# Batch-axis attention: who writes the weight blocks, and which engine forms the normalised rows

## The reference

```python
def _L1_attn_ref(query, ...):           # query: L=16, N=128, E=256
    H = 16; L, N, E = query.shape; d = 16; scale = d ** (-0.5)
    q = split_heads(query @ q_proj.T + q_bias) * scale      # (N, H, L, d)
    k = split_heads(query @ k_proj.T + k_bias)
    v = split_heads(query @ v_proj.T + v_bias)
    scores = einsum('nhld,nhkd->nhlk', q, k)
    scores = where(tril(ones((L, L))), scores, -10000.0)
    attn = softmax(scores, axis=-1)
    ctx = einsum('nhlk,nhkd->nhld', attn, v)
    return ctx.transpose(2, 0, 1, 3).reshape(L, N, 256) @ out_proj.T + out_bias
```

## Time and profile before

| | us |
|---|---|
| device time, three runs | 1278.31, 1285.85, 1287.44 (median 1285.85) |
| profiled execution, its own time | 1279.03 |
| its span in the trace | 1277.2 |
| the batch-axis block in it | from about 712 to 848 |
| of it, the weighing: start of the lane writes to the end of the last strip | 789.0 to 816.8 |
| of it, the output projection and normalisations | 817.7 to 848.2 |

### The profile page before, as it was taken

The page is one execution under the profiler, slowest core; times in us unless marked ns, Lnnn a source line. Parts: engine busy times, 40 slices in busy tenths (PEclk is TensorE's granted clock), DMA queues, the critical chain, the costliest instruction groups (busy, mean ns, idle before and its releaser), DMA issues. The chain is left out here.

```text
span 1277.2 us, 23930 instructions
## 1 busy us (share of the span) xinstructions
PE 1136.4 (89%) x8865; PEld 731.3 (57%) x8880; DVE 909.6 (71%) x2118; ACT 570.3 (45%) x1521; POOL 283.8 (22%) x343
## 2 busy tenths in 40 slices
PE   9799999899998999889899987779999999879965
PEld 3587888677763333335456545657777776334422
DVE  1799999599995787848997598654458778843325
ACT  4111121444434666646453335527777676222212
POOL 5000000022220111221343213630000000147742
PEclk9899999999998999999999998989999999989987
DMA  7011131300002232134000000129000000549557
GB/s 246 6 54 55 54 82 57 98 2 2 2 2 74 76 104 91 59 58 88 1 1 1 1 2 1 68 74 328 20 18 25 23 18 28 166 137 279 88 114 260
DMA packets 82335, 91.39 MB, mean 72 GB/s; under 512 B 25360, under 2 KB 65830, under 8 KB 81958
## 3 DMA queue, kind: packets, MB, share of 16 engines
q1 hardware_dynamic: 73820, 76.90, 20.0%
q0 software_dynamic: 6272, 9.25, 3.9%
q10 hardware_dynamic: 2128, 3.71, 0.8%
HBM read 68.00 MB, written 21.84 MB: 70 GB/s over the span
## 5 line engine op out<-in xcount | busy, mean ns | idle before, releaser
L401 DVE TENSOR_REDUCE gqa_x_slots<-gqa_scores 128x8 f32<-128x1024 f32 x64 | 78.4, 1226 | 30.2 <-PE gqa_scores L288 21.2
L1564 DVE TENSOR_REDUCE mla_neg_max<-mla_scores 128x8 f32<-128x1024 f32 x32 | 39.2, 1225 | 77.8 <-PE mla_scores L1429 52.2
L1511 ACT ACTIVATE mla_probs<-mla_scores,mla_neg_max 128x128 f32<-128x128 f32 x256 | 90.1, 388 | 0.0
L358 ACT ACTIVATE gqa_expT<-gqa_scoresT 128x1024 f32<-128x1024 f32 x64 | 65.5, 1024 | 49.8 <-PE gqa_scoresT L309 49.8
L309 PE MATMUL gqa_scoresT<-gqa_x_slotsT,gqa_keys 32*128 32x512 f32 x256 | 73.4, 645 | 10.9 <-issue 4.9
L2246 PE MATMUL ttt_z_ps<-ttt_prod,ident 128*128 128x256 f32 x288 | 68.6, 394 | 8.6 <-DVE ttt_prod L2322 8.6
L288 PE MATMUL gqa_scores<-gqa_keys_bd,xT 32*128 32x512 f32 x256 | 72.7, 659 | 2.7 <-DVE gqa_x_slots L401 1.4
L1419 PE MATMUL mla_q_ps<-xT,mla_merged_home 128*128 128x128 f32 x512 | 64.4, 280 | 1.6 <-PEq L63 1.6
L2246 PEld LDWEIGHTS ttt_z_ps<-ttt_prod,ident 128*128 128x128 f32 x288 | 53.6, 194 | 21.0 <-DVE ttt_prod L2322 14.3
L2253 PE MATMUL ttt_w_ps<-ttt_prod,ttt_neg_ident 128*128 128x144 f32 x448 | 60.2, 295 | 4.9 <-DVE ttt_prod L2355 4.9
L2253 PEld LDWEIGHTS ttt_w_ps<-ttt_prod,ttt_neg_ident 128*128 128x128 f32 x448 | 59.6, 198 | 5.9 <-DVE ttt_prod L2355 5.3
(11 more groups left out here) (461 smaller groups left out, 2743.4 us busy)
## 6 DMA issues: line engine op xcount, KB each, us to landing
moe_w_gu<-in_moe_w_gu SPq DMA_DIRECT2D x24, 384.0 KB
gqa_keys_bd<-in_gqa_keys_bd SPq DMA_DIRECT2D x16, 512.0 KB, 3.3
moe_w_dn<-in_moe_w_down SPq DMA_DIRECT2D x24, 192.0 KB
moe_sums<-moe_zeros SPq DMA_DIRECT2D x2, 2176.0 KB, 11.5
xT<-in_x_feat SPq DMA_DIRECT2D x4, 512.0 KB
ttt_k_by_head<-ttt_k_feat SPq DMA_DIRECT2D x8, 256.0 KB, 4.2
ttt_k_seq<-ttt_k_by_head SPq DMA_DIRECT2D x4, 512.0 KB, 5.3
x_tok<-in_mla_woT SPq DMA_DIRECT2D x8, 256.0 KB, 3.2
```

The costliest lines, as they stand in the source:

```text
L358: nc.scalar.activation(expT[:, k % 2, 2 * u:2 * u + 2, :], scoresT[:], ACT.Exp, scale=HD ** -0.5).then_inc(exp_ready, 1)
L401: nc.vector.tensor_reduce(x_slots[:, b % 2, :, c * NJ + 2 * half:c * NJ + 2 * half + 2, HD].rearrange("p g j -> p j g"), scores[:, of].rea ...
L1511: ins = nc.scalar.activation(probs[:, k % NB, e, i, :], scores[:, k % 2, e, i, :], ACT.Exp, bias=neg_max[:, k % 2, e, i:i + 1], accum_out= ...
```

## The change

It has two parts.

1. Lanes 4 to 7 of every block are written by DMA. GpSimd clears those four lanes of each buffer once (buffer 0 at the start of the block, buffers 1 and 2 after its last tail copy and once the last sums that read that space are done). SyncE waits until all pairs are kept, and then issues four DMAs for each strip, each from the 16 partitions r, r+8, ... of `turned` to the same partitions of lane r, 2 KB a partition. Since only those partitions are ever written, the zeros stay. VectorE writes three lanes in place of four, ScalarE one in place of three, GpSimd none. TensorE waits for the DMAs of its buffer in place of `pool_laid`. The fetch of the next stage's weights stays behind these issues on SyncE.
2. The normalised row is formed by ScalarE: VectorE only makes `shift` = -mean x rstd (128 x 1), and ScalarE computes total x rstd + shift. `vector_begin` of an entry now waits until ScalarE has formed the row of the entry two before, because it overwrites the same `total`. On ScalarE the row of n is formed ahead of the copy to `xT` of n-1.

```diff
--- before.py
+++ after.py
@@ -191,6 +191,30 @@
 
         eng.wait_ge(self.kept, self.count)
         eng.wait_ge(self.turn_copied, self.count)
+
+
+class NormOnScalar(Norm):
+
+
+
+    def __init__(self, nc, ctx, tag, keep, turned_psum, place, count):
+        super().__init__(nc, ctx, tag, keep, turned_psum, place=place, count=count)
+        self.shift = ctx.enter_context(nc.sbuf_tensor(f"{tag}_shift", [P, 1], F32))
+        self.shift_ready = new_semaphore(nc, keep, f"{tag}_shift_ready")
+
+    def vector_begin(self, eng, order, b, y):
+        need(eng, self.norm_ready, b)
+        super().vector_begin(eng, order, b, y)
+
+    def vector_end(self, eng, b):
+        need(eng, self.rstd_ready, b + 1)
+        self.nc.vector.scalar_tensor_tensor(self.shift[:], self.mean_var[:, 0:1], -1.0, self.rstd[:], ALU.mult, ALU.mult).then_inc(self.shift_ready, 1)
+
+    def normalise(self, eng, b):
+        need(eng, self.shift_ready, b + 1)
+        need(eng, self.kept, b)
+        need(eng, self.turn_ready, b)
+        self.nc.scalar.activation(self.normed[:], self.total[:], ACT.Identity, bias=self.shift[:], scale=self.rstd[:]).then_inc(self.norm_ready, 1)
 
 
 class CrossFirst:
@@ -873,9 +897,10 @@
         shifted, exp_ready, probs_ready, tail_ready = sem("shifted"), sem("exp_ready"), sem("probs_ready"), sem("tail_ready")
         pads_clear = sem("pads_clear")
         turn_ready, turn_kept, weighed, att_kept = sem("turn_ready"), sem("turn_kept"), sem("weighed"), sem("att_kept")
-        dve_laid, act_laid, pool_laid = sem("dve_laid"), sem("act_laid"), sem("pool_laid")
+        dve_laid, act_laid, lanes_clear = sem("dve_laid"), sem("act_laid"), sem("lanes_clear")
+        lanes_loaded = [sem(f"lanes_loaded{n}") for n in range(EB)]
         out_ready, chain, merged = sem("out_ready"), sem("chain"), sem("merged")
-        norms = [Norm(nc, ctx, f"ba_n{k}", keep, turned_ps[:, k, 0:D], place=lambda n, k=k: 2 * n + k, count=L // 2) for k in range(2)]
+        norms = [NormOnScalar(nc, ctx, f"ba_n{k}", keep, turned_ps[:, k, 0:D], place=lambda n, k=k: 2 * n + k, count=L // 2) for k in range(2)]
 
         QUARTERS = T * L // 512
         PROJECTIONS = [(name, g, c) for g in range(QUARTERS) for name in "qk" for c in range(DH)]
@@ -883,27 +908,33 @@
         pairs_of = lambda i: probs[:, i].rearrange("p a v m r -> p (a v) m r")
         has_keys = lambda i: (2 * i // (L // QUARTERS) + 1) * 2 * DH
 
-        lane, BY_DVE = inputs.lane, 4
+        lane, BY_DVE, BY_DMA = inputs.lane, 3, 4
         lane_of = lambda s, r: by_lane[s % EB][:, r].rearrange("p x l -> p (x l)")
 
         block = ctx.enter_context(nc.Block())
 
         @block.sync
         def _(sp):
+            sp.wait_ge(turn_kept, PAIRS)
+            for s in range(STRIPS):
+                sp.wait_ge(lanes_clear, min(s + 1, EB))
+                need(sp, weighed, s - EB + 1)
+                for r in range(R - BY_DMA, R):
+                    sp.dma_start(by_lane[s % EB][r::R, r], turned[r::R, s]).then_inc(lanes_loaded[s % EB], 16)
             sp.wait_ge(weighed, STRIPS - 1)
             fetch(sp, latent.merged_loads, merged)
 
         @block.gpsimd
         def _(pool):
             nc.gpsimd.memset(values[:, :, :, 1, :], 0.0).then_inc(pads_clear, 1)
+            nc.gpsimd.memset(by_lane[0][:, R - BY_DMA:R], 0.0).then_inc(lanes_clear, 1)
             for i in range(TAILED):
                 n = slots(i)
                 pool.wait_ge(probs_ready, i + 1)
                 nc.gpsimd.tensor_copy(pairs_of(i)[:, :, n:L, :], pairs_of(i)[:, :, n - 1, :].unsqueeze(2).to_broadcast([P, 4, L - n, R])).then_inc(tail_ready, 1)
-            pool.wait_ge(turn_kept, PAIRS)
-            for s in range(STRIPS):
-                need(pool, weighed, s - EB + 1)
-                nc.gpsimd.tensor_scalar(lane_of(s, R - 1), turned[:, s].rearrange("p x l -> p (x l)"), lane[:, R - 1:R], None, ALU.mult).then_inc(pool_laid, 1)
+            for n in range(1, EB):
+                pool.wait_ge(summed, 4 * PAIRS - 2 * (EB - 1 - n))
+                nc.gpsimd.memset(by_lane[n][:, R - BY_DMA:R], 0.0).then_inc(lanes_clear, 1)
             for n in range(L):
                 norms[n % 2].gpsimd(pool, n // 2)
 
@@ -959,7 +990,7 @@
                 n = s % EB
                 pe.wait_ge(dve_laid, s + 1)
                 pe.wait_ge(act_laid, s + 1)
-                pe.wait_ge(pool_laid, s + 1)
+                pe.wait_ge(lanes_loaded[n], 16 * BY_DMA * (s // EB + 1))
                 need(pe, att_kept, s + 1 - NT)
                 for c in range(DH):
                     for th in range(2):
@@ -1079,7 +1110,7 @@
             keep_values(12, VG)
             def lay_out_lanes(s):
                 need(act, weighed, s - EB + 1)
-                for r in range(BY_DVE, R - 1):
+                for r in range(BY_DVE, R - BY_DMA):
                     ins = nc.scalar.mul(lane_of(s, r), turned[:, s].rearrange("p x l -> p (x l)"), lane[:, r:r + 1])
                 ins.then_inc(act_laid, 1)
 
@@ -1091,7 +1122,10 @@
                     lay_out_lanes(s + 2)
                 keep_attended(s)
             for n in range(L):
-                norms[n % 2].scalar(act, n // 2)
+                norms[n % 2].normalise(act, n // 2)
+                if n >= 1:
+                    norms[(n - 1) % 2].scalar(act, (n - 1) // 2)
+            norms[(L - 1) % 2].scalar(act, (L - 1) // 2)
             for norm in norms:
                 norm.done(act)
```

## The result

| | before | after |
|---|---|---|
| device time, median (20 runs each, same chip) | 1281.41 us | 1287.70 us |
| lowest and highest | 1275.45, 1297.15 | 1278.84, 1298.35 |
| ratio after/before | | 1.0046, 95% interval 1.0024 to 1.0068 |
| profiled execution: span, time | 1277.2, 1279.03 | 1277.8, 1279.56 |
| weighing: first lane write to end of strip 7 | 789.0 to 816.8: 27.8 | 785.5 to 811.0: 25.5 |

The change makes the kernel slower by 0.5%, some 6 us (3 to 9). I had forecast 3 us less: 1283.0, in a range that holds 1287.7, with the wrong sign. The two spans differ by only 0.6 us because the profiled execution of after reached the weighing 3.5 us earlier, in stages that the change doesn't touch; so I compare stretches.

What follows compares the result with a forecast made beforehand. TensorE waiting for GpSimd's lanes bounds the weighing, VectorE's laps the normalisations. Part 1's -8.6 and part 2's +5.6 sum to -3.0 us: 1283 from a median of 1285.85, range 1273 to 1291.

Steps and rivals of the forecast that it cites:

- What bounds the kernel now: Weighing: TensorE waits for GpSimd's lanes, some 12 of 27.8 us waiting and slow clock; normalisations: VectorE's 16 laps set them.
- The issues: Weighing: SyncE's 32 DMA issues at 0.48 us each, nearly tied with TensorE's strips; part 1 gains 8.6 us.
- The dear end: Weighing: issues at 0.64 us give a last landing at 810.9 and an end at 812.9, a gain of 3.9.
- Landing, lanes, clearing: Weighing: landing 2.0 us, VectorE's three lanes 1.75, ScalarE's one 0.65, GpSimd's clearing 0, with 1.7 as its other end.
- Part 2: Normalisations: ScalarE's row still lies inside VectorE's lap, which goes from 1.70 to 2.05 us; +5.6 us, between 5.3 and 6.0.
- "if" of that step: Normalisations: lap 2.08 us, or 2.03 if `shift`, waiting for one semaphore in place of three, comes 0.05 earlier; 2.05 taken.
- A: Rival, weighing: TensorE's clock falls in the 1.4 us ahead of strip 0; +2.5 us, so -0.5 in all, 1285.4; 13%.
- B: Rival, weighing: slow landing through reuse of three buffers; at 4.2 us +4.5 in all, 1290.4; 12%, shared with dear issues.
- C: Rival, normalisations: ScalarE's row is hidden and VectorE's lap falls to 1.44 us; -11.5 in all, 1274; 7%.
- the ring that spoke against it: Normalisations: add(n+2) follows shift(n) and needs row(n), with one `total` per parity, leaving VectorE no work between.
- D: Rival, normalisations: TensorE's clock falls, its 1.24 us a lap become 2.33; +3.9, so +0.9 in all, 1287; 8%.
- The sum: Whole kernel: -8.6 + 5.6 = -3.0 us, 1283 against the median 1285.85; 60% for this forecast.

Runs made afterwards that it cites:

- e1: Part 1 alone (lanes by DMA, normalised rows by VectorE as before) on the kernel before: 1274.51 us against 1278.15, ratio 0.9978; weighing 26.2 us.
- e3: e1 with two of each strip's four DMAs issued by GpSimd in place of SyncE: 1270.98 us against 1280.37 for before, ratio 0.9897; weighing 19.2.
- e7: Part 2 alone, with two total tiles for each Norm: 1276.75 us against 1280.37 for before, ratio 0.9999; normalisations 33.4, laps 1.80.
- e4: e1 with three lanes a strip by DMA in place of four and two by ScalarE: 1271.66 us, ratio 0.9949 to before; weighing 24.2.
- e8: e7 with GpSimd making an entry's root ahead of the copy of the row before: 1278.96 us against 1280.37 for before, ratio 0.9980; normalisations 30.7.
- e10: e8 with TensorE turning the row of three entries before in place of two: 1269.90 us against 1281.53 for before, ratio 0.9914; normalisations 24.8.
- e5: e1 with each DMA copying 16 neighbouring partitions in place of every eighth: 1273.20 us in one run; weighing 27.0.
- e9: The whole change with each strip's four DMAs issued two by SyncE, two by GpSimd: 1279.19 us against 1281.53 for before, ratio 0.9977; weighing 19.1.

## Why the prediction was wrong, step by step

**What bounds the kernel now.** Right. With GpSimd out of the lanes (e1, e3) the waits for it are gone, and the slow first strip with them.

**The issues: the step that failed.** "With 0.04 between two I take 0.48 ... and keep 0.64 as the other end." The rows offered 0.44 and 0.60, and I chose by the look of the transfer. It was 0.589, 0.63 start to start, and four issues took 2.53 us, over the 1.94 that the prediction named as a sign of being wrong. The other three steps of that sum held, so the miss can be booked in full. From the first write, forecast: 31 x 0.48 = 14.9 to the last issue, 2.0 to land, 1.95 for the strip, 0.4 for hand-over and slips: 19.2. Measured: last issue at 807.0, that is 21.5 after the first, of which 31 x 0.63 = 19.5 is plain and 2.0 are three hold-ups; landing 1.8; 0.2; strip 1.95: 25.5. So 4.6 of the 6.3 us are the price of the issue, 2.0 the hold-ups that no step had, and -0.3 the rest. At 0.48 four issues lie just under a strip of TensorE, at 0.63 they lie above it: the choice between two neighbouring rows decided which engine binds, and 0.15 us was paid 31 times. e3 shows this on the chip: with the issuing shared, part 1 gives 8.6, which is the forecast for it.

**The dear end too was not dear enough.** With 0.64 I had the end at 812.9 and part 1 at -3.9. Measured -2.2: the difference of 1.7 is the hold-ups (2.0), less what 0.64 overstates (31 x 0.01 = 0.3). A bound worked out from medians of single issues leaves out what a row of 32 meets; the maximum in such a row (here 1.23) is a term of its own.

**Landing, lanes, clearing.** Forecast 2.0, measured 1.8. VectorE's three lanes 1.75, measured 1.758. ScalarE's 0.65, measured 0.715, hidden. The two memsets beside the softmax took 1.8 us each and held up nothing, so the value 0 for them was right. The Trainium skill (SBUF — State Buffer, Who interferes with whom) says that a VectorE instruction with two SBUF inputs doesn't contend with a GpSimd instruction that only writes. The trace agrees as far as it tests this: the one VectorE instruction with two SBUF inputs that overlaps a memset (L1166 of after, by 0.2 us) takes 0.69 us in both kernels. The weight fetch behind the issues started at 808.7, as soon as strip 6 was weighed; it held up nothing.

**Part 2.** The mechanism was right in all its parts: the add behind the shift, the row between them, VectorE idle and released by ScalarE. Lap 2.05, measured 2.10; 14 x 0.05 = 0.7 covers the difference of 5.6 to 6.2. The 0.05 is the "if" of that step, a shift that would come earlier with fewer waits. It didn't: 2.08 was the other value given. That GpSimd's own loop hides behind it was right (e7: 1.80).

**The rivals.** A (clock falls ahead of strip 0): wrong, the clock is 1.00 from 785.5 to 811 with 1.68 us of idle time ahead of strip 0. It did fall in e4, behind a gap of 2.3 us. B (slow landing): the landing decided nothing, but its outcome came (+4.0 for +4.5) by another way, the dear issues, to which I gave a share of B's 12%. C (VectorE gets the faster lap of 1.44): wrong for this change, by the ring that spoke against it; e7, e8 and e10 show that three rings had to be opened before VectorE got it, and then it got 1.27. I had carried the gaps of the old lap over; they were hand-overs, not work. D (clock in the normalisations): 0.98 in that window in place of 1.00; only the last turn shows it (0.69 in place of 0.44).

**The sum.** -2.2 + 6.2 = +4.0 by the traces, +5.9 (3.1 to 8.7) by the ratio. That 1287.7 lies in the range, and the ratio within 1%, is owed to the width of both and not to the sum, whose sign was wrong. The mistake in the chances follows from the step: part 2 was a nearly sure loss of 5.6, and part 1 a gain between 0 and 9 that hung on one price. The sum changes sign at an issue of 0.58 us (789.05 + 31 x 0.58 + 2.0 + 1.94 + 0.2 = 811.2, the end at which part 2 eats the gain), and 0.58 lies inside the rows that I had. The forecast should have worked out that point, as it did for the landing; 60% for -3 was too much.

**Open.** That rows of a DMA wait behind an instruction packet is read from the packets' times. That the packet also makes SyncE's next issue longer was argued from its place (three of three in after, beside each late landing). Neither was tried: no kernel here removes the packets. Nor was the issue price of GpSimd tried for all 32. And e10 gains 11.0 us (7.3 to 14.6) by its runs but 6.6 by its normalisations. In its one trace the stages ahead of the weighing are 5.8 us shorter than in before, where no edit touches them; over the traces here the weighing starts anywhere from 783.3 to 791.7. What the rest of e10's gain is, no trace shows.

## What to carry to other kernels

When DMAs replace an engine's work, price the issuing engine like any other: issues a tile times the dearest plausible issue, set against the engine that is to be fed, and where the two lie close, share the issuing with an idle engine. An instruction moved off the full engine gains nothing while the next one waits for its result: walk the ring (which tile is overwritten, who stands ahead of it in whose program), and expect a second and third ring behind the first. Opening them cost a second tile and two changes of order here, and turned a loss of 6 us into a gain of 6.6.

## What the runs showed of the hardware

- An issue by SyncE of a DMA from 16 partitions to 16, 2 KB each, in SBUF: 0.589 us median, 0.63 start to start in a row; neighbouring partitions don't make it cheaper (0.589 in e5). By GpSimd 0.483. Landing 1.8 us.
- Beside a packet of instructions (16 KB, 0.9 to 1.5 us) a landing takes up to 2.8 us (4.1 in e4) and SyncE's next issue 0.9 to 1.2 (1.8 in e4), three times in 22 us of small DMAs; in after, one of a DMA's 16 rows starts only when that packet has ended. GpSimd's issues stay at 0.48 in e9 while one of SyncE's beside them takes 1.47; their landings grow too.
- TensorE's strips are read as 1.95 us each, but where two follow without a wait they start 1.75 apart (two in a row 3.70): eight would take 14.2, not the 15.5 of the forecast.
